# A sparse-expert layer: adding the dense matrix W into every expert's matrix instead of multiplying by it separately

## What is computed

```python
logits = clip(xt @ gate_w.T, -50, 50)            # 8 experts
top_w, top_idx = top_k(logits, 2)
rw = softmax(top_w)
# every expert has a sparse 512 x 512 matrix (4096 entries at places that all experts share)
out = xt @ W.T + contrib.T                       # contrib: rw-weighted sum over the token's two experts
x = layernorm(x + out)
```

## Time and profile before

| | |
|---|---|
| median of 3 runs | 4557.28 us |
| lowest and highest | 4544.99, 4560.86 us |
| span of the profiled execution | 4554.9 us |
| TensorE busy | 4154.4 us, 91% of the span |
| VectorE, ScalarE, GpSimd busy | 1926.6, 1328.0, 280.2 us |
| TensorE clock granted, mean | 0.947 of full speed |

### The profile page before, as it was taken

The page is one execution under the profiler, slowest core; times in us unless marked ns, Lnnn a source line. Parts: engine busy times, 40 slices in busy tenths (PEclk is TensorE's granted clock), DMA queues, the critical chain, the costliest instruction groups (busy, mean ns, idle before and its releaser), DMA issues. The chain is left out here.

```text
span 4554.9 us, 60589 instructions
## 1 busy us (share of the span) xinstructions
PE 4154.4 (91%) x20058; PEld 2811.2 (62%) x20059; DVE 1926.6 (42%) x6611; ACT 1328.0 (29%) x2941; POOL 280.2 (6%) x304
## 2 busy tenths in 40 slices
PE   7899999899999988958999999889999997699996
PEld 7667777577777765425555555545555554577775
DVE  4343334344434343144444444444454454634435
ACT  1233233233333334112222322223333333412221
POOL 2230000200000004130000000000000000000000
PEclk8999999899999997977999999989999998899998
DMA  6521111221111104430000000000000001000000
GB/s 216 167 47 41 37 46 52 91 84 49 44 39 39 39 30 155 138 121 23 1 2 1 2 1 2 17 22 3 3 3 4 3 3 38 19 19 9 18 18 37
DMA packets 83751, 191.59 MB, mean 42 GB/s; under 512 B 22416, under 2 KB 27792, under 8 KB 82456
## 3 DMA queue, kind: packets, MB, share of 16 engines
q0 software_dynamic: 31360, 94.52, 6.7%
q1 hardware_dynamic: 52192, 94.53, 6.1%
HBM read 138.56 MB, written 50.47 MB: 41 GB/s over the span
## 5 line engine op out<-in xcount | busy, mean ns | idle before, releaser
L1686 ACT ACTIVATE probsT_c<-bank 128x512 f32<-128x512 f32 x256 | 152.8, 597 | 585.1 <-PE bank L1550 585.1
L1686 ACT ACTIVATE probsT_y<-bank 128x512 f32<-128x512 f32 x256 | 152.8, 597 | 463.0 <-PE bank L1547 463.0
L1566 PE MATMUL bank<-probsT_y,v_y 128*32 128x256 f32 x1024 | 265.7, 386 | 0.0
L1776 DVE TENSOR_REDUCE mx_y<-bank 128x2 f32<-128x512 f32 x288 | 187.4, 688 | 174.7 <-PE bank L1529 172.1
L446 PE MATMUL bank<-wo_s,work_s 128*128 128x512 f32 x512 | 229.0, 598 | 7.1 <-ACT work_s L478 3.8
L446 PE MATMUL bank<-wo_x,work_x 128*128 128x512 f32 x512 | 227.2, 594 | 5.1 <-ACT work_x L478 3.8
L1566 PE MATMUL bank<-probsT_c,v_c 128*32 128x128 f32 (+1 forms) x1024 | 210.8, 332 | 0.0
L478 ACT ACTIVATE work_s<-bank 128x512 f32<-128x512 f32 (+1 forms) x224 | 104.0, 464 | 356.6 <-PE bank L435 175.1
L478 ACT ACTIVATE work_x<-bank 128x256 f32<-128x256 f32 (+1 forms) x240 | 109.4, 459 | 323.4 <-PE bank L435 188.4
L1545 PE MATMUL bank<-qT_c,kT_c 64*128 64x256 f32 x512 | 196.2, 383 | 4.0 <-DVE negT_c L1769 0.7
L583 DVE CUSTOM_DVE_ANT_0 work_x<-bank,work_x 128x256 f32<-128x256 f32 x256 | 97.8, 419 | 221.2 <-issue 221.2
(11 more groups left out here) (416 smaller groups left out, 8840.5 us busy)
## 6 DMA issues: line engine op xcount, KB each, us to landing
wq_lo_s<-wq_lo_s POOLq DMA_DIRECT2D x64, 512.0 KB, 3.6
wq_lo_x<-wq_lo_x POOLq DMA_DIRECT2D x64, 512.0 KB, 3.5
expert_rows<-table_zero SPq DMA_DIRECT2D x20, 512.0 KB, 14.1
work_m<-expert_rows SPq DMA_DIRECT2D x40, 256.0 KB, 2.6
expert_products<-work_m POOLq DMA_DIRECT2D x40, 256.0 KB, 2.7
expert_table<-table_zero SPq DMA_DIRECT2D x16, 512.0 KB, 13.7
weights_m<-expert_table SPq DMA_DIRECT2D x4, 2048.0 KB, 9.6
ug_rows<-in_L_ffn_W_gate SPq DMA_DIRECT2D x9, 512.0 KB, 4.0
```

The source lines that it names most:

```text
L1566: last = pe.matmul(b[r:r + VW, col + q0:col + SEQ], v[:, par, k, kh, :], probsT[:, h % PTS, k * SEQ + q0:(k + 1) * SEQ], start=(k == 0), s ...
L1686: act.activation(probsT[:, h % PTS, :], scoreT[h % 2][:, :], ACT.Exp, scale=SCALE)\
L1776: dve.tensor_reduce(mx[:, :, h], b[:, :].rearrange("p (t k) -> p t k", t=TILES), AX.X, ALU.max)\
```

## The change

- The dense product goes: `dense_pair` on PE with its second turning of x, `dense_share` and the second `stage_pair` on ACT, `add_x` on DVE, and the semaphores between them.
- ACT's `regroup` goes. DVE does columns 256 to 511 in its place, now as an addition: `join_chunk(cc)` writes `M = stage + WT`, W repeated for each of the eight experts. POOL's copy of columns 0 to 255 becomes the same addition.
- On DVE, `join_chunk(0)` and `join_chunk(1)` stand after the first `stage_pair`, ahead of the other three rounds of logits; `join_chunk(2)` and `join_chunk(3)` stand after the last `stage_pair`, ahead of the reading of the last logits.
- In the finish, the first of the two gated additions takes `chip.x` as its base rather than `total`.

```diff
-            def dense_pair(it):
...
-            with pe.Fori(0, BATCH // 2 - 1) as it:
-                transpose_pair(it + BATCH // 2)
-                dense_pair(it)
-            transpose_pair(BATCH - 1)
-            pe.wait_ge(s["dense_copied"], 2 * BATCH - 2)
-            pe.wait_ge(s["xT_copied"], 4 * BATCH)
+            pe.wait_ge(s["xT_copied"], 2 * BATCH)
...
-            pe.wait_ge(s["product_copied"], SLOTS_OF_TOKENS + 2)
-            dense_pair(BATCH // 2 - 1)
...
-            def regroup(cc):
-                act.wait_ge(chunk_loaded[cc % 2], 16 * (cc // 2 + 1))
-                copy(M[:, cc, :, DIM // 2:], stage[:, cc % 2, :].rearrange("p (r e) -> p e r", e=EXPERTS)[:, :, DIM // 2:])\
-                    .then_inc(s["chunk_used"], 1)
...
+            def join_chunk(cc):
+
+                dve.wait_ge(s["wT_copied"], cc + 1)
+                dve.wait_ge(chunk_loaded[cc % 2], 16 * (cc // 2 + 1))
+                dve.tensor_tensor(M[:, cc, :, DIM // 2:],
+                                  stage[:, cc % 2, :].rearrange("p (r e) -> p e r", e=EXPERTS)[:, :, DIM // 2:],
+                                  WT[:, cc, DIM // 2:].unsqueeze(1).to_broadcast([P, EXPERTS, DIM // 2]), ALU.add)\
+                   .then_inc(s["chunk_used"], 1)
+
             stage_pair(0)
             dve.memset(rotary.pos[:, :, :], 0.0).then_inc(rotary.cleared, 1)
             dve.drain().then_inc(s["logits_read"], 1)
+            join_chunk(0)
+            join_chunk(1)
             with dve.Fori(1, BATCH // 2) as it:
                 dve.wait_ge(s["logits_ready"], it)
                 dve.memset(tick, 0.0)
                 stage_pair(it)
                 read_logits(it - 1)
+            join_chunk(2)
+            join_chunk(3)
             dve.wait_ge(s["logits_ready"], BATCH // 2)
             read_logits(BATCH // 2 - 1)
...
-            with dve.Fori(0, BATCH - 2) as it:
-                add_x(it)
             dve.drain().then_inc(s["product_copied"], 2)
...
-            with dve.Fori(0, BATCH // 2 - 1) as it:
+            with dve.Fori(0, BATCH // 2) as it:
                 finish_pair(it)
-            for n in (BATCH - 2, BATCH - 1):
-                add_x(n)
-            finish_pair(BATCH // 2 - 1)
...
             for cc in range(DC):
+                pool.wait_ge(s["wT_copied"], cc + 1)
                 pool.wait_ge(chunk_loaded[cc % 2], 16 * (cc // 2 + 1))
-                pool.tensor_copy(M[:, cc, :, 0:DIM // 2], stage[:, cc % 2, :].rearrange("p (r e) -> p e r", e=EXPERTS)[:, :, 0:DIM // 2])\
+                pool.tensor_tensor(M[:, cc, :, 0:DIM // 2],
+                                   stage[:, cc % 2, :].rearrange("p (r e) -> p e r", e=EXPERTS)[:, :, 0:DIM // 2],
+                                   WT[:, cc, 0:DIM // 2].unsqueeze(1).to_broadcast([P, EXPERTS, DIM // 2]), ALU.add)\
                     .then_inc(s["chunk_used2"], 1)
```

More of the change, by code:

```diff
@@ L909, in experts @@
     slot_expert_int = carve(SLOTS_OF_TOKENS).bitcast(INT32)
-    tick, ticks = carve(1), carve(2 * TILES)
+    tick = carve(1)
     rank = chip.const[:, C_RANK:C_RANK + EXPERTS].unsqueeze(1).to_broadcast([P, NTILE, EXPERTS])
@@ L922, in experts @@
             "xT_ready", "xT_copied", "logits_ready", "logits_read", "margin_ready", "exp_ready", "sent_ready",
-            "ranks_ready", "dest_ready", "slots_known", "dense_ready", "dense_copied", "slot_turned",
+            "ranks_ready", "dest_ready", "slots_known", "slot_turned",
             "slot_copied", "slot_done", "product_copied", "stats_ready", "x_ready")}
@@ L1072, in _ @@
             copy(gateT.rearrange("p c e -> p (c e)"), logits_bank[:, 0:DC * EXPERTS]).then_inc(s["wT_copied"], 1)
-            with act.Fori(0, BATCH // 4) as it:
+            with act.Fori(0, BATCH // 2) as it:
                 transposed(it)
[L1075 to L1087, removed]
             act.wait_ge(s["margin_ready"], 1)
             act.activation(d, d, ACT.Exp).then_inc(s["exp_ready"], 1)
[L1091 to L1105, removed]
             rotary.sines(act)
@@ L1111, in _ @@
                     copy(slotT[:, k % 2, :, :].rearrange("p c q -> p (c q)"), turn_bank[k % 2][:, :]).then_inc(s["slot_copied"], 1)
-            dense_share(BATCH // 2 - 1)
             act.wait_ge(s["stats_ready"], 1)
@@ L1214, in _ @@
             rotary.angles(dve, chip)
-            def add_x(it):
-                dve.wait_ge(s["dense_copied"], it * TILES + TILES + 2)
-                dve.memset(tick, 0.0)
-                rows = total[:, bass.ds(it * TILES, TILES), :]
-                dve.tensor_tensor(rows, rows, chip.x[:, bass.ds(it * TILES, TILES), :], ALU.add)
-                dve.drain()
-            with dve.Fori(0, BATCH - 2) as it:
-                add_x(it)
             dve.drain().then_inc(s["product_copied"], 2)
@@ L1243, in finish_pair @@
                     rows = [total[:, bass.ds(n * TILES + tile, 1), :] for tile in range(TILES)]
-                    for i, gate in enumerate((g1, g2)):
+                    before_ = [chip.x[:, bass.ds(n * TILES + tile, 1), :] for tile in range(TILES)]
+                    for i, (gate, base) in enumerate(((g1, before_), (g2, rows))):
                         for tile in range(TILES):
                             last = dve.scalar_tensor_tensor(rows[tile], fetched[:, u, tile, i:i + 1, :],
-                                                            gate[:, bass.ds(n * TILES + tile, 1)], rows[tile], ALU.mult, ALU.add)
+                                                            gate[:, bass.ds(n * TILES + tile, 1)], base[tile], ALU.mult, ALU.add)
                         if i == 1:
```

## The result

The changed kernel takes 4576.41 us (median of 5 runs, 4570.33 to 4585.53), where the kernel before took 4556.75 us beside it (5 runs, 4544.99 to 4560.86). The ratio is 1.0057, with a 95% interval of 1.0037 to 1.0077. It is slower by more than the 0.3% that this measurement can tell. The prediction was 4570 us, with a range of 4553 to 4584. The range holds the result, but the likeliest case, a time within 0.3% of before, did not come; the loss is 20 us where 12.6 was forecast.

The account below looks back on a forecast made before the run. Outside TensorE's slot loop, logits rounds, GpSimd's scatter issues and the finish's fetches and sums bound the expert block, not TensorE. +16 us for logits less 3.4 gives +12.6 us: 4570 us predicted, range 4553 to 4584.

Parts of the forecast that it names:

- the dense product at 0: Scatter and finish: removing some 57 us of TensorE work gains nothing, being hidden; rival that it was not: 1 in 100.
- The scatter, -3.0: Scatter stage: six VectorE additions of x no longer stretch GpSimd's issues, -3.0 us, bounds 0 and 5.2.
- the finish, -0.4: Finish: the last two additions of x no longer stretch a GpSimd issue, -0.4 us.
- The start of the slot loop: Slot loop's start: TensorE idle for 40 us ahead of it costs at most 1 us, hidden in the rounding.
- The price of an addition: Joins ahead of the scatter: 6.55 us on GpSimd (4.7 to 8.8), 4.3 on VectorE (2.3 to 4.3).
- The exclusion: Logits rounds: VectorE's and GpSimd's additions with SBUF inputs exclude each other, so their times add up.
- the walk: Logits rounds, timed instruction by instruction: last logits at 1776.0 against 1760.24, +15.8 us; +2.2 by lower bounds, +24.7 by upper.
- what shifts with the block keeps its length: Routing, scatter and slot loop shift with the logits; the slot loop stays at 156 us.
- Theory B: From the experiments: TensorE's missing dense work lengthens the later narrow attentions, to about 1820 us instead of 1806.
- The dearer addition: Joins: stride multiplies GpSimd's cost to 8.8 us each, +21 us, 4579 us; decides from about 6.9 us; chance 0.17.
- No exclusion: Joins: VectorE's run beside GpSimd's, only copies held up; +1.7 us, 4559 us; chance, with prices near lower bounds, 0.17.
- The faster one: Logits rounds: the two copy waits (2.8 and 3.6 us) vanish with nothing in their place; -9.8 us, 4547 us; chance 0.06.

Follow-up runs that it names:

- e1: Against the kernel after: joins replaced by the plain copies of before, W added nowhere, dense product still gone; 4564.01 us, ratio 0.9984 to the kernel before.
- e3: Against the kernel after: VectorE's joins read their half of W from PSUM instead of SBUF; 4565.06 us, ratio 0.9992 to the kernel before.
- delayed executions: Kernel before with one, two or four VectorE buffer clearings behind the last logits; 4564.05, 4584.2 and 4576.15 us.
- the delay of 8.9 us: Kernel before with two VectorE buffer clearings behind the last logits, also called twice-delayed; 4584.2 us, ratio 1.0035 to the kernel before.

## Why the prediction was right or wrong

*What bounds the kernel, and the dense product at 0.* Right, and shown: with 54.7 us less of TensorE work, `e1` has 3 us less in the scatter, 0.3 in the slot loop and finish, and a logits stage (50.0) inside the spread of the kernel before.

*The scatter, -3.0, and the finish, -0.4.* Right: -3.0 and -2.3 us in the two pairs of profiles, and 42.0 to 42.2 us in every kernel without `add_x`; loop and finish -0.4 and -1.7.

*The start of the slot loop, at most 1 us.* About right: +0.5 and +1.1. TensorE comes to it after 55 us of idleness (the prediction had 40), at the low clock: 0.50 in the scatter window.

*The price of an addition.* GpSimd 6.55 us forecast, 5.5 measured; VectorE 4.3 forecast, 3.9 measured. GpSimd's contiguous addition is 4.5 us for 2048 elements, a little less than twice the 2.37 of the earlier trace rows, and the step adds 1.0, not 1.81, so the two costs do not simply add.

*The exclusion.* Right, and its cause shown by `e3`. The order was wrong in detail. I had GpSimd run two additions in a row ahead of VectorE's joins, and so chunk 2 asked for only at 1733.6; in fact the engines alternate, chunk 0 was done at about 1725, and GpSimd's third addition fell between the two copies of the first round and cost a third wait. The cheaper additions in turn freed the second round (1749.4, with GpSimd done at 1747.6), whose copies wait for nothing and end 5.5 us earlier than in the walk, though those of the first end 1.3 later. The walk gave the last logits at 1776.0; they came at 1771.7, with the last round at 9.8 us (low clock) instead of the 6.7 taken, so VectorE's last two joins are covered; that last stretch is 1.2 us longer than in the walk. The 4.3 us by which the walk was too long are the difference of these misses, and in part luck. Its lower end, +2.2 us, does not follow from the walk: with 4.7 and 2.3 us GpSimd's fourth addition begins at 1742.8, 0.2 us ahead of the copies (1743.0), which by the same rule wait for it, and the walk ends at 1766.8, +6.6.

*The sum for the block.* Forecast +12.6, measured +9.0 and +15.4. The walk's +16 was measured as +11.9 and +18.3, and that difference is the kernel before's own: 54.7 or 48.1 us. Against the mean of its five stages, 49.1, the walk's part is +17.4. A single profile of before did not show that; that the sum is near the first ledger is in part the choice of that profile.

*The step that failed: what shifts with the block keeps its length.* The prediction said of the routing, scatter and slot loop that they shift with the logits, and took the same of all behind the block without a word. The two narrow attentions took 13.6 and 8.4 us more. In the first pair of profiles the block's +9.0 alone is inside the bound of 0.3%, and the attentions carry the loss outside it.

That the clock has a large part in this is measured, over unchanged instructions. In the table the length of the two follows the time at the low clock: over the 14 executions the correlation is 0.93, and the fitted line is 1718 us + 0.44 us for each us at 0.5. It gives 10.5 of the 13.6 us and 3.8 of the 8.4; the rest has no cause shown. Runs of one kernel say the same: the 25 of the kernel before in the first set reach over 29 us, and the longer ones have the lower mean clock (correlation -0.90).

What sets the time at the low clock stays open. That it is the moment of arrival is not shown: the delayed executions have 212 to 237 us of it, against 206 and 211, but the 25 runs of the kernel before differ among themselves by more, with no shift at all: their mean clock goes from 0.945 to 0.951, an estimated 55 us more or less of the whole span at 0.5. Theory B, TensorE's missing work, has more for it than the sums say (1820.0 us on average in the nine executions without the dense product, 1812.9 in the five with it). The difference lies in the first attention alone: 911.8 to 918.6 us without the dense product, 903.5 to 912.8 with it, against means of 905.0 and 904.7 in the second. In the first attention the clock record of each of the five shows 10 stretches at 0.5 that begin in it, that of each of the nine 12 or 13, at nearly the same distances from the block's start; eight of the nine have one 276 to 282 us behind it, where none of the five has any. No run puts work in the place of the dense product to test this. It would not explain the second attention, where the delay of 8.9 us has the longest of all, 913.7. Open as well is why the kernel before had two medians 18 us apart on one chip: its mean clock differed by 0.001, and by the spread within a set that is worth an estimated 4 us.

*The rivals.* The dearer addition did not come (5.5 us is below the 6.9 from which it decided), though its time of 4579 is nearer to the result than the sum is. No exclusion is refuted for the kernel as it stands and is `e3`. The faster one needed the waits of before to vanish with nothing in their place; in the kernel after two copies and a join waited instead. Even `e1`, which has no joins, has one long copy (4.05 us, behind a copy of GpSimd), with 50.0 us instead of 54.7.

## What to carry to other kernels

When two engines can't read SBUF at the same time, count for each short instruction between their long ones a whole wait, and let them alternate in the walk; a short copy is the worst thing to leave there, and an operand in PSUM or an idle third engine takes it out. Before costing a change from waits in one profile, ask whether they would be there if one engine came 1 us earlier, and profile the baseline more than once: here the same code took 44.9 to 54.7 us. And if most of the program is TensorE work whose clock moves between two levels, stages that nobody touched can give or take as much as the change itself: here from 2 to 23 us beside the first profile of before.

## What was not expected of the hardware

- Identical TensorE instructions (4355 and 3934 of them) took 1806 to 1829 us with what stands between them, the longer the more time the granted clock was at 0.5 (206 to 245 us). The executions without the dense product have 12 or 13 such stretches in the first attention, those with it 10; the cause was not looked into further.
- Two waiting engines alternated at SBUF in the kernel after, one instruction each: additions of 5.3 to 5.4 us on GpSimd and single instructions of VectorE, seven in a row from the first join to the second copy of x.
- The address step costs the engines different amounts: 1.6 us of VectorE's addition of 2048 elements and 1.0 us of GpSimd's.
- ScalarE stood for 10.6 and 11.3 us at a wait that the trace calls remote, in one execution of the twice-delayed kernel only.
